# Batch 0's expert layer, computed by tiles of tokens sorted by expert instead of densely

## What is computed

```python
x = _layernorm(x + attention_8_heads(x))            # causal, head size 16
h = x + mla_attention(rmsnorm(x))                   # causal, 16 heads of size 8
def moe(x, gate_w, gate_b, W1, b1, W2, b2):         # x: rmsnorm(h), 4 experts, hidden size 512
    logits = x @ gate_w.T + gate_b
    onehot = one_hot(argmax(logits, axis=-1), 4)
    h = relu(einsum('btd,ehd->bteh', x, W1) + b1)
    y = einsum('bteh,edh->bted', h, W2) + b2
    return einsum('bted,bte->btd', y, onehot)
out = _layernorm(x + h + moe(...))
```

## Time and profile before

| what | value |
|---|---|
| median of the runs | 613.81 us |
| the profiled execution's own time | 617.44 us |
| its span | 615.7 us |
| TensorE matmul busy | 549.5 us (89%) |
| VectorE, ScalarE, GpSimd busy | 416.2, 350.7, 157.3 us |
| mean granted TensorE clock | 0.955 |
| moved by DMA | 25.64 MB, mean 42 GB/s |

### The profile page before, as it was taken

The page is one execution under the profiler, slowest core; times in us unless marked ns, Lnnn a source line. Parts: engine busy times, 40 slices in busy tenths (PEclk is TensorE's granted clock), DMA queues, the critical chain, the costliest instruction groups (busy, mean ns, idle before and its releaser), DMA issues.

```text
span 615.7 us, 10700 instructions
## 1 busy us (share of the span) xinstructions
PE 549.5 (89%) x3869; PEld 255.0 (41%) x3885; DVE 416.2 (68%) x1063; ACT 350.7 (57%) x673; POOL 157.3 (26%) x217
## 2 busy tenths in 40 slices
PE   6577799888899988898989999999999999999993
PEld 3323234434433333332333334543545445347662
DVE  4396989768888869786878887776666721643144
ACT  4413267754765767745767776656556666653330
POOL 9631012353534155342111221301101102201000
PEclk9877899997999999996989999999999999999998
DMA  3992023005022001020010101001000000010000
GB/s 117 178 210 91 21 70 104 2 1 200 17 71 62 1 25 56 26 79 28 2 54 2 53 2 54 2 2 53 2 3 2 1 2 1 2 35 2 0 15 20
DMA packets 27846, 25.64 MB, mean 42 GB/s; under 512 B 7377, under 2 KB 24401, under 8 KB 27538
## 3 DMA queue, kind: packets, MB, share of 16 engines
q1 hardware_dynamic: 27410, 24.17, 14.4%
q0 software_dynamic: 384, 0.79, 0.7%
HBM read 17.30 MB, written 7.34 MB: 40 GB/s over the span
## 4 chain that ended last, share of the span: by engine, by line
PE 69%; DVE 8%; SPq 8%; ACT 7%; DMA 3%; issue 3%; POOL 1%; DVEq 0%; ACTq 0%; POOLq 0%
PE ps L1227 15%; PE ps L1210 12%; PE ps L1306 10%; PE ps L1362 10%; PE ps L1189 9%; ACT pr L1382 5%; DVE mparts L1604 4%; SPq L913 4%; PE ps L1292 3%; SPq L967 2%; PE ps L1286 2%; DMA qs<-nparts 2%; PE ps L1238 2%; PE ps L1267 2%; PE ps L1184 1%
## 5 line engine op out<-in xcount | busy, mean ns | idle before, releaser
L1382 ACT ACTIVATE pr<-ps 128x512 f32<-128x512 f32 (+1 forms) x480 | 249.9, 554 | 167.1 <-PE ps L1210 137.0
L1604 DVE TENSOR_REDUCE mparts<-ps 128x1 f32<-128x512 f32 (+3 forms) x480 | 279.9, 630 | 89.1 <-PE ps L1189 87.5
L1210 PE MATMUL ps<-qs,ks 64*128 64x512 bf16 (+7 forms) x560 | 153.3, 338 | 18.3 <-ACT pr L1382 10.1
L1189 PE MATMUL ps<-ks,qs 61*128 61x512 bf16 (+7 forms) x576 | 155.4, 347 | 6.9 <-DMA qs<-nparts 3.7
L1227 PE MATMUL ps<-pr,vs 128*32 128x512 f32 (+3 forms) x1152 | 125.0, 507 | 1.5 <-ACT pr L1382 0.3
L1083 POOL TENSOR_SCALAR_AFFINE_SELECT pr<-pr 128x512 f32<-128x512 f32 x96 | 60.9, 634 | 227.7 <-ACT pr L1382 227.6
L1210 PEld LDWEIGHTS ps<-qs,ks 64*128 64x128 bf16 (+1 forms) x576 | 44.6, 96 | 136.9 <-ACT pr L1382 97.5
L1306 PE MATMUL ps<-w,work 128*128 128x128 f32 x512 | 67.7, 283 | 0.0
L1189 PEld LDWEIGHTS ps<-ks,qs 61*128 61x128 bf16 (+1 forms) x576 | 51.0, 100 | 37.8 <-DVE mparts L1604 19.6
L1362 PE MATMUL ps<-feat,w 128*128 128x512 f32 x128 | 65.8, 621 | 0.0
L1306 PEld LDWEIGHTS ps<-w,work 128*128 128x128 f32 x512 | 60.2, 191 | 9.5 <-issue 9.3
(11 more groups left out here) (138 smaller groups left out, 501.3 us busy)
## 6 DMA issues: line engine op xcount, KB each, us to landing
qs<-scr0q SPq DMA_DIRECT2D x48, 64.0 KB, 2.3
qs<-scr1q SPq DMA_DIRECT2D x84, 32.0 KB
ks<-scr1k SPq DMA_DIRECT2D x84, 32.0 KB
ks<-scr0k SPq DMA_DIRECT2D x36, 64.0 KB, 2.2
scr0q<-parts SPq DMA_DIRECT2D x4, 384.0 KB, 2.9
scr0k<-parts SPq DMA_DIRECT2D x4, 384.0 KB, 3.8
scr1q<-parts SPq DMA_DIRECT2D x4, 384.0 KB, 2.6
scr1k<-parts SPq DMA_DIRECT2D x4, 384.0 KB, 2.6
```

The lines of the kernel that those rows point to most:

```text
L1189: last = pe.matmul(bank[:, h, :], queries(F, 0, h0 + h, i * P, P), keys(F, 0, h0 + h, 512 * c, w), start=not diagonal, stop=True, skip_gro ...
L1210: last = pe.matmul(to[:, h, :], keys(F, 3, h0 + h, j * P, P), queries(F, 3, h0 + h, qb * 512 + lo, n), start=True, stop=True)
L1382: act.activation(pr[:, st % PSLOTS, h0:h0 + nh, 0:STEPS[st][3]], scores_at(F, v), ACT.Exp, scale=GROUPS[F][0].scale).then_inc(exped, 1)
L1604: dve.tensor_reduce(mparts[:, F % SLOTS, h0:h0 + nh, i, c], maxes_at(F, u), AX_X, ALU.max).then_inc(taken, 1)
```

## The change

Batch 1 stays as it was. For batch 0, both blocks' one-hot choices go through a small matmul with a triangular matrix (`rank`), which counts for each token the earlier ones of the same expert. VectorE turns the counts into a destination row per token and into the weight rows per tile (`places`, 12 small operations). Each expert's rows begin at a multiple of 128, so 8 tiles of tokens become 8 + 4 - 1 = 11 tiles, whatever the choice. Eight indirect DMAs from GpSimd scatter the tokens' rows (`xn`, 64 KB each) to DRAM (`rows_in_order`), three DMAs from SyncE bring them back sorted (`sorted`, 704 KB in all), and per tile two indirect DMAs from GpSimd fetch that tile's W1 with b2 (2560 bytes for each of 128 rows) and W2 with b1 (2064 bytes), in two buffers by turns. Per tile TensorE does 1 transpose, 4 matmuls and 4 matmuls, ScalarE 5 operations, VectorE 1, and SyncE stores 64 KB. At the end eight indirect DMAs gather the rows back (`collect`), and VectorE adds the residual (`collected`). On SyncE a table and a filling of `rows_in_order` (704 KB, DRAM to DRAM) follow the expert weights; GpSimd makes the constants (`rank_made`, position 1.3).

The diff, cut to its core:

```diff
+SORTED = [(0, (0, 1))]
+DENSE = [(b, i) for b in range(B) for i in range(2) if not any(b == sb and i in si for sb, si in SORTED)]
...
+def rows_of_tiles(s):
+    return len(tokens_of(s)) + E - 1
...
+def by_rows(s):
+    n, J = len(tokens_of(s)), rows_of_tiles(s)
+    out = [("rank", s), ("places", s)] + [("scatter", s, t) for t in range(n)]
+    out += [("fetch", s, j, w) for j in range(2) for w in range(2)]
+    out += [("sorted", s, p) for p in range(-(-J // PIECES))]
+    for j in range(J):
+        out += [("row_turn", s, j), ("row_feat", s, j), ("tile_hidden", s, j), ("tile_relu", s, j), ("tile_out", s, j),
+                ("tile_sum", s, j), ("tile_store", s, j)]
+        if j + 2 < J:
+            out += [("fetch", s, j + 2, w) for w in range(2)]
+    out += [("collect", s, t) for t in range(n)]
+    return out + [("collected", SORTED[s][0], i) for i in SORTED[s][1]]
...
+            if (b, i) in DENSE:
+                add("result", spread(experts(b, i), *EXPERTS[b][i]))
             add("result", spread(results(b, i), *RESULTS[b][i]))
+    for s in range(len(SORTED)):
+        add("rows", spread(by_rows(s), *BY_ROWS[s]))
     for F in range(NF):
...
+BY_ROWS = [(8.45, 11.5)]
...
+COSTS = {"rank": (PE, 0.7), "places": (DVE, 2.8), "scatter": (POOL, 1.2), "fetch": (POOL, 1.2), "sorted": (SP, 0.4),
+         "row_turn": (PE, 0.2), "row_feat": (ACTE, 0.3), "tile_hidden": (PE, 1.2), "tile_relu": (ACTE, 1.2), "tile_out": (PE, 1.2),
+         "tile_sum": (DVE, 0.35), "tile_store": (SP, 0.4), "collect": (POOL, 1.2), "collected": (DVE, 0.7), "rank_made": (POOL, 1.2),
...
+LANDS_LATER = {"scatter": 2.5, "fetch": 4.5, "collect": 3.0, "sorted": 2.0, "weights": 4.0, "moe_weights": 10.0, "store": 1.0}
...
+        w1_row, w2_row = HID + C, HID + HC
+        fetched_w1 = parts[:, :, :, :].rearrange("p s a n -> p (s a n)").bitcast(F32)
+        xs = work[:, 1024:1024 + P * (TB + E - 1)].rearrange("p (j c) -> p j c", c=C)
+        tile_hid = work[:, 0:1024].rearrange("p (s c n) -> p s c n", s=2, c=HC)
+        tile_x = work[:, 2432:2688].rearrange("p (s n) -> p s n", s=2)
+        tile_y = work[:, 2688:2944].rearrange("p (s n) -> p s n", s=2)
...
+                sp.dma_start(numbers[:, :], a["numbers"]).then_inc(rows_set, 16)
+                any_rows = a["x"].rearrange("b t c -> (b t) c")[0:P * (TB + E - 1), :]
+                sp.dma_start(rows_in_order[:, :], any_rows).then_inc(rows_set, 16)
+            def sorted_rows(s, p):
+                j = slice(PIECES * p, min(PIECES * p + PIECES, rows_of_tiles(s)))
+                sp.wait_ge(scattered, 16 * len(tokens_of(s)))
+                if p == 0:
+                    sp.wait_ge(done["lo"], nth("lo", 15))
+                sp.dma_start(xs[:, j, :], rows_in_order.rearrange("(j p) c -> p j c", p=P)[:, j, :]).then_inc(sorted_in[p], 16)
+            def tile_store(s, j):
+                sp.wait_ge(done["tile_sum"], nth("tile_sum", s, j))
+                sp.dma_start(rows_out[j * P:(j + 1) * P, :], tile_y[:, j % 2, :]).then_inc(y_stored[j % 2], 16)
...
+            def scatter(s, t):
+                if t == 0:
+                    pool.wait_ge(rows_set, 32)
+                    pool.wait_ge(done["places"], nth("places", s))
+                b, blocks = SORTED[s]
+                pool.wait_ge(done["hat"], nth("hat", b, blocks[t // 4]))
+                pool.indirect_dma_start(rows_in_order[:, :], IndirectOffsetOnAxis(ap=place_of[:, t:t + 1], axis=0),
+                                        xn[:, tokens_of(s)[t], :], None).then_inc(scattered, 16)
+            def fetch(s, j, w):
+                if j == 0 and w == 0:
+                    pool.wait_ge(done["places"], nth("places", s))
+                    pool.wait_ge(done["rotate"], nth("rotate", 15, 1))
+                    for M in range(16 - PARTS, 16):
+                        pool.wait_ge(stored[M % PARTS], stored_value(M))
+                if j >= 2 and w == 0:
+                    pool.wait_ge(done["tile_sum"], nth("tile_sum", s, j - 2))
+                to = (cos, sin)[j % 2][:, 0:w2_row] if w else fetched_w1[:, j % 2 * w1_row:(j % 2 + 1) * w1_row]
+                pool.indirect_dma_start(to, None, a[("w1_rows", "w2_rows")[w]],
+                                        IndirectOffsetOnAxis(ap=row_of[:, j:j + 1], axis=0)).then_inc(fetched[j % 2], 16)
+            def collect(s, t):
+                if t == 0:
+                    J = rows_of_tiles(s)
+                    pool.wait_ge(y_stored[0], 16 * ((J + 1) // 2))
+                    pool.wait_ge(y_stored[1], 16 * (J // 2))
+                pool.indirect_dma_start(xn[:, tokens_of(s)[t], :], None, rows_out[:, :],
+                                        IndirectOffsetOnAxis(ap=place_of[:, t:t + 1], axis=0)).then_inc(collected_in[t // 4], 16)
...
+                elif kind == "rank":
...
+                    pe.wait_ge(done["rank_made"], 1)
+                    pe.wait_ge(done["pick"], nth("pick", b, blocks[-1]))
+                    wait_bank(*step)
+                    counts = side(*step)[:, 0:(n + 1) * E]
+                    chosen = choice[:, 0:n + 1, :].rearrange("p t e -> p (t e)")
+                    pe.matmul(counts, below[:, :], chosen, start=True, stop=False, skip_group_check=True)
+                    for k in range(1, n + 1):
+                        last = pe.matmul(counts[:, k * E:], every[:, :], chosen[:, 0:(n + 1 - k) * E],
+                                         start=False, stop=k == n, skip_group_check=True)
+                    last.then_inc(done["rank"], 1)
+                elif kind == "row_turn":
+                    s, j = args
+                    pe.wait_ge(sorted_in[j // PIECES], 16)
+                    wait_bank(*step)
+                    pe.transpose(side(*step)[:, 0:P], xs[:, j, :], ident[:, :]).then_inc(done["row_turn"], 1)
+                elif kind == "tile_hidden":
+                    s, j = args
+                    pe.wait_ge(done["row_feat"], nth("row_feat", s, j))
+                    pe.wait_ge(fetched[j % 2], 32 * (j // 2 + 1))
+                    wait_bank(*step)
+                    for c in range(HC):
+                        first = j % 2 * w1_row + c * P
+                        last = pe.matmul(side(*step)[:, c * P:(c + 1) * P], fetched_w1[:, first:first + P], tile_x[:, j % 2, :],
+                                         start=True, stop=True)
+                    last.then_inc(done["tile_hidden"], 1)
+                elif kind == "tile_out":
+                    s, j = args
+                    pe.wait_ge(done["tile_relu"], nth("tile_relu", s, j))
+                    wait_bank(*step)
+                    for c in range(HC):
+                        last = pe.matmul(side(*step)[:, 0:C], tile_hid[:, j % 2, c, :], (cos, sin)[j % 2][:, c * C:(c + 1) * C],
+                                         start=c == 0, stop=c == HC - 1)
+                    last.then_inc(done["tile_out"], 1)
...
+                elif kind == "row_feat":
+                    s, j = args
+                    act.wait_ge(done["row_turn"], nth("row_turn", s, j))
+                    if j >= 2:
+                        act.wait_ge(done["tile_hidden"], nth("tile_hidden", s, j - 2))
+                    act.activation(tile_x[:, j % 2, :], side("row_turn", s, j)[:, 0:P], ACT.Identity,
+                                   scale=norm_w[:, 1:2]).then_inc(done["row_feat"], 1)
+                elif kind == "tile_relu":
+                    s, j = args
+                    act.wait_ge(done["tile_hidden"], nth("tile_hidden", s, j))
+                    if j >= 2:
+                        act.wait_ge(done["tile_out"], nth("tile_out", s, j - 2))
+                    for c in range(HC):
+                        last = act.activation(tile_hid[:, j % 2, c, :], side("tile_hidden", s, j)[:, c * P:(c + 1) * P], ACT.Relu,
+                                              bias=(cos, sin)[j % 2][:, HID + c:HID + c + 1])
+                    last.then_inc(done["tile_relu"], 1)
...
-                    if (b, i, c) == (0, 0, 0):
+                    if (b, i, c) == (*DENSE[0], 0):
                         act.wait_ge(done["lo"], nth("lo", 15))
+                        J = rows_of_tiles(len(SORTED) - 1)
+                        act.wait_ge(y_stored[0], 16 * ((J + 1) // 2))
+                        act.wait_ge(y_stored[1], 16 * (J // 2))
...
+                elif kind == "tile_sum":
+                    s, j = args
+                    dve.wait_ge(done["tile_out"], nth("tile_out", s, j))
+                    if j >= 2:
+                        dve.wait_ge(y_stored[j % 2], 16 * (j // 2))
+                    first = j % 2 * w1_row + HID
+                    dve.tensor_tensor(tile_y[:, j % 2, :], side("tile_out", s, j)[:, 0:C], fetched_w1[:, first:first + C],
+                                      ALU.add).then_inc(done["tile_sum"], 1)
+                elif kind == "collected":
+                    b, i = args
+                    dve.wait_ge(collected_in[i], 16 * 4)
```

(2 more changed lines are left out.)

153 lines of the change are left out of this document (140 added, 13 removed).

## The result

The changed kernel takes 619.0 us (median of 20 runs, 616.2 to 624.0), the kernel before in the same rounds 614.2 us: ratio 1.0077, 95% interval 1.0054 to 1.0101. It is slower by 0.8%. The forecast was 586.0 us, range 573 to 606.

The account below looks back on a forecast made before the run. TensorE alone was taken to set the pace where batch 0's experts run. The terms -71.3 + 28.7 + 9 + 6 = -27.6 us, off the median of 613.8, gave 586 us, range 573 to 606.

Parts of the forecast that it names:

- What is removed: -71.3: Batch 0's 8 dense experts among attention, 8.9 us each on TensorE, come off the time: -71.3 us.
- What the experts had been filling: +9: Waits reopen without filler: 5.4 us for bare F8, 2.7 for half of F11, 1 at F7's end.
- What is added: +28.7: TensorE gains 11 tiles at 2.5 us, 27.3 in all, and about 1.4 for `rank`'s nine small matmuls.
- hand-overs +6: Tiles cross between TensorE and ScalarE; 8 of 22 hand-overs stay uncovered at about 0.76 us each.
- GpSimd: "I count nothing": Masks queued behind fetch pairs on GpSimd wait up to 2.4 us; nothing counted, bound 24 masks x 1 us.
- SyncE: "with a wide lead; nothing": 14 more SyncE DMAs with row maxima and loads behind them, issued with a wide lead in F9 and F10: nothing.
- The fetches: Weight fetch pairs land in some 5.5 us, 6.5 us per tile, so tiles are likely not late.
- No packing: Rival, chance 0.12: tiles are added to the bare pace in F8 to F10, about 600 us.
- The clock: Rival, chance 0.08: gaps in F8 to F11 lower TensorE's clock to a mean of 0.9, 11 us more, 597.
- late fetches: Rival, chance 0.11: tile hidden steps stand at the wait on `fetched`, 11 times, holding attention; about 630 us.
- Full gain: Rival, chance 0.10: the planner finds other fillers and hides the hand-overs, about 574 us.
- not saved where it counts: Rival, chance 0.02: tiles slip behind F11 or batch 1's first Relu waits for the last store; within 0.2%.

Follow-up runs that it names:

- run 4: The floor: kernel before with batch 0's experts left out altogether and the list planned anew (output not right); 578.7 us, ratio 0.9444 to the kernel before.
- run 14: The new list with all 38 indirect DMAs made plain ones of the same bytes, sorting by expert left out (chip D); 594.6 us, ratio 0.9664.
- run 15: The new list unaltered, measured again on chip D; 601.3 us, ratio 0.9762 to the kernel before.
- run 9: The changed kernel unaltered, measured again on chip C; 619.5 us, ratio 1.0094 to the kernel before.
- run 10: Changed kernel with F9's row maxima moved ahead of load 11 and the sorted reloads on SyncE, same as run 1 but on chip C; 629.1 us, ratio 1.0216.
- run 1: Changed kernel with F9's row maxima moved ahead of load 11 and the sorted reloads on SyncE, chip A; 616.0 us, ratio 1.0014.
- the new list: Changed kernel planned anew: load 11 after F9's maxima and sorted rows, sorted rows after those maxima, gathers after x12(1,0), later wanted places; 602.6 us, ratio 0.9819.
- run 2: Changed kernel with batch 0's gathers behind x12(1,0), and block 0's sum and norm behind batch 1's last choice; 608.7 us, ratio 0.9907.
- run 13: The new list with each of GpSimd's first 12 indirect DMAs waiting until the one before has landed (chip D); 615.1 us, ratio 1.0013.
- run 3: Changed kernel with all 38 indirect DMAs made plain ones of the same bytes, sorting by expert left out; 606.8 us, ratio 0.9884.
- run 12: Run 11's order with all 38 indirect DMAs made plain ones, sorting by expert left out (chip C); 605.1 us, ratio 0.9839.
- run 5: Changed kernel with SyncE's order F9's maxima, sorted rows, then load 11 (chip B); 620.4 us, ratio 1.0101.
- run 11: Changed kernel with SyncE's order F9's maxima, sorted rows, then load 11, same as run 5 but on chip C; 618.5 us, ratio 1.0072.
- run 8: First measurement of the new list, on chip B; 602.6 us, ratio 0.9819 to the kernel before.

## Why the prediction was wrong

From the forecast to the changed kernel it is 33 us; slower than before had been given a chance of 0.11. By the floor and the plain twins they divide so:

| term | forecast | measured | from |
|---|---|---|---|
| batch 0's experts gone | 614 to 564 | 614 to 579 | run 4: +15 |
| tiles and hand-overs, best list, plain DMAs | +22 | +16 | run 14: -6 |
| indirection | 0 | +7 | runs 14, 15: +7 |
| the changed kernel's list instead of the new one | 0 | +18 | runs 9, 15: +18 |

The forecast's 564 is -71.3 for the experts and four groups' waits of 5.4 us given back; its 22 are the rest of its sum. The rows compare medians of different series, which is good to 2 us or so; how they add up (33 or 34) says no more.

**What is removed: -71.3, the first step that failed.** It rests on the sentence that TensorE alone sets the pace and that what the experts occupy on it is what they cost. The size was too large: TensorE's busy time falls by 549.5 - 497.0 = 52.5 us in the floor run, though attention has a lower clock there in places; the sum for experts alone, 60.2, was the better guess. And only 35.7 come off the time, because without them TensorE no longer sets the pace alone. The floor's profiled execution is 41.8 us shorter than that of the kernel before: 2.4 up to F8, 15.8 in F8, 4.1 in F9, 15.3 in F10, 4.2 in F11, nothing in the end. So "attention's own pace" is not one number: F10's is F6's, but F9's is 10 us longer, since a bare F8 is over before VectorE's maxima for F9 are out and F9's scores wait for them on their way through SyncE and a DMA. Dense experts had kept F8 long enough for this. I saw the gap fillers only as 5.4 us a group.

**What the experts had been filling: +9.** Right in kind, too small, and in the wrong place: F8 bare is 33 us as forecast (33.0 in the floor run, 32.0 to 36.4 in the runs other than the changed kernel), F10 36.6 where 37 was forecast. F9 took 52.9 instead of 37.

**What is added: +28.7, and hand-overs +6.** About right, even high: TensorE's busy time rises from 497.0 to 520.3 us in run 14, 23.3, and the time by 16. (The nine matmuls of `rank` at 0.2 would be 1.8 and not 1.4, which is of no weight.) ScalarE's small step took 0.36 to 0.42 us where 0.37 was taken. In the changed kernel TensorE's weight loads waited for a tile's rows 1.1 us and for its Relu 1.6 us in all; 8 times 0.76 was taken.

**GpSimd: "I count nothing".** The issue was priced well: 0.94 to 1.13 us, 1.27 with the gap, where 1.2 was taken. What was missed is the queue behind it, though its bound (24 masks by 1 us) was written down: eight gathers in one piece keep TensorE waiting 5.2 us for a mask, in the one half-group on which the end depends. And what no row could show: the joint stall.

**SyncE: "with a wide lead; nothing".** In the list F9's row maxima stood behind 24 DMAs of load 11 and behind a wait for the scatters. Taken away by hand on chip C it brought only 1 us (the stall keeps the maxima late), and half taken away, with the sorted rows left behind load 11, it cost 10 there (run 10 against 9). The lead was not wide; it was none at F9, and I hadn't looked at which step comes next in SyncE's list.

**The fetches.** No wait of TensorE for a fetch shows in the changed kernel: ahead of the hidden steps its weight loads stood 3.4 us in all. So the pairs were not late, as said. Run 14's issues show the size of one plain fetch:

```profile
parts<-in_w_rows POOLq DMA_DIRECT2D x11, 320.0 KB, 3.3
cos<-in_w_rows POOLq DMA_DIRECT2D x6, 258.0 KB, 3.5
```

The Trainium skill, DMA: Bandwidth & Descriptors, section Anatomy of one DMA, gives 2.8 us as an estimate for the first, as the prediction said; 3.3 was measured. My 5.5 was for a pair; from these rows I estimate a plain pair at two issues of 0.55 and a landing of 3.5, so it was too high for plain DMAs. For indirect ones the page of the profile has no landing time.

**The rivals.** No packing (600, 0.12) was the nearest by its reason: tiles add to a bare pace, but the bare pace was misjudged. The clock (597, 0.08) is real as a follower: 0.81, 0.84 and 0.74 in F8, F9 and the first half of F11. After the stall it was at 0.50, the lower level, from 421 to 430 us with TensorE at work. That is below the 0.95 which was to show the forecast wrong. By the Trainium skill, TensorE: Matmul & The Clock Gate, section HAM oscillation, waits between groups of matmuls throttle the clock again and again; the trace agrees, with these three stretches and their waits on one side and F10, where TensorE is busy 96% and the clock 1.00, on the other. The rival that ends slower (late fetches, 0.11) was right on the side and wrong on the place: not the wait on `fetched`, but row maxima, masks and releases held up at the burst. Full gain and not saved where it counts did not come; the latter's thought, that only some stretches count, is right, and F11's first half is the one.

**Left open.** Why bursts on GpSimd delay the releases by TensorE's matmuls: the traces show them late, not what holds them, and since a matmul's end is modelled not even whether the matmuls or only their signals are late. Why the same kernel had none of it in the trace of run 1 and 9 us in that of run 10 (10.1 and 19.3 us to the maxima): up to the burst the two traces run alike, 4.7 us apart. Which of the new list's changes brought its 18 us, beyond the 5.7 of the gathers' place, wasn't tried one by one. Whether a pause of under 1.5 us between indirect DMAs is enough wasn't tried.

## What to carry to other kernels

Before counting work off the busiest engine, ask in each stage what it covered: here the dense experts kept F8 long enough for F9's row maxima to be ready in time, and what I had down as 71 us of work was worth 36. The kernel's own planner had put it at 34 (expectation of experiment 4); an assumed cost list that exists is worth asking before summing. When a fixed list gets a new kind of step, read what stands right behind each new step on every queue, GpSimd's and SyncE's too, and plan the list anew with those needs: that turned +0.8% into about -2%. And look for the one moment on which the end hangs (here the first half of F11); a wait ahead of it costs in full, however idle the engines look.

## What the runs showed of the hardware

An indirect DMA of 128 rows occupied GpSimd 0.94 to 1.13 us with 0.3 us between two, a plain one of the same bytes 0.55. The Trainium skill, DMA: Bandwidth & Descriptors, section Anatomy of one DMA, calls the generation of descriptors small; here 12 indirect DMAs in one piece occupied GpSimd for 15 us. While the 8 scatters and 4 fetches were issued 0.3 us apart, waits for TensorE's matmuls ended late, mostly several engines' together, with 1.4 to 12.5 us as the longest, in 12 of the 14 traces that have this burst; the two without are of runs 1 and 2. With 1.5 us or more between the DMAs (run 13), and with plain DMAs (runs 3, 12, 14), none did. Nor did the eight gathers in F11, which are as close behind one another (0.30 us), show it in any trace. SyncE's own DMA issues slowed in part: the second twelve of load 11 took 6.5, 5.1 and 5.8 us in the three traces of the changed kernel where 4.0 is usual, while the first twelve, beside the burst too, took 4.0 to 4.4. ScalarE's wait in the stall repeats to a tenth for one list (12.5 us in three traces of the changed kernel, 5.3 in runs 5 and 11, 3.1 in runs 8 and 15) and changes with the list, and one kernel had 616.0 us on one chip and 629.1 on another.
